# FFN's end with own buffers, and the first groups of a decoder-like layer in another order

## The chip, the cores and the metric

One core of a Trainium2 chip runs one program written by hand in Bass: every engine has its own list of instructions, and semaphores order them. The metric is the device time of one execution in microseconds.

## The reference

Input x is 32 sequences of 32 tokens of 256 values, 1024 rows in all; each sequence has a context of 257 rows of 256 values. Three layers are added to x in turn, each on layer-normalised rows:

```python
x = x + cross_attention(layernorm(x), ctx, ctx)   # one head: softmax(q k^T) v, q, k, v with biases
x = x + favor_attention(layernorm(x))             # 16 heads of 64, phi(x) = exp(x.W - |x|^2/2)/sqrt(128),
                                                  # causal within a sequence, divided by its sum, then Wo
x = x + ffn(layernorm(x))                         # gelu(bitlinear(x, w1)), bitlinear(., w2)
# bitlinear: activations rounded to 8 bits by their row's largest value, weights to -1, 0, 1 times a scale
```

## The kernel before, in words

The 1024 rows are 8 groups of 128 rows (NG = 8), four sequences in each. TensorE is called PE, VectorE DVE, ScalarE ACT, GpSimd POOL and the sync engine SP. The kernel has three parts: the front (cross attention of all groups, 0 to about 82 us), the middle (the features and products of the 16 heads) and the end (output projection and FFN).

**Front.** For each group g, with the lines at which its steps stand:

- `x_norm(g)` (DVE, L774) normalises x. For pairs of groups j, `xT(j)` transposes it (PE L1208), ACT takes the high part of the result (L493) and DVE the low part (L780), and `qk(j)` multiplies it with M = Wq Wk^T (PE L1220, copied by ACT L500). Products that need precision are made of three matmuls of high and low parts.
- `scores(g)` (PE L1242) multiplies with the context transposed (cT), `softmax_bias(g)` (DVE L834, three instructions from L837) takes the largest score, `exp(g)` (ACT L509), `pTt(g)` (PE L1255) transposes, `pTc(g)` (ACT L517) copies, `avm(g)` (PE L1276) multiplies with the context (cn), and `avc(g)` (DVE L842) adds the last key and copies. The four products of the last keys are `last_keys` (PE L1265).
- `avTt(g)`, `avT(g)` (PE L1287, ACT L523, DVE L827) transpose the result, `wv(g)` (PE L1295) multiplies it with Wv, and `x1(g)` (DVE L851) adds it to the rows kept in `res`. Into these POOL has added the bias bv (`add_bias`, L351) before.
- `stats(1, g)`, POOL's `rstd` (L358) and `x2_norm(g)` (DVE L857) normalise again. `nT(g)` (PE L1310, ACT, DVE) transposes, and `values(g, 0)` and `values(g, 1)` (PE L1319) make the two halves of the values of the next attention with the weight wv, whose high and low parts are `split_wv` (ACT L559) and `split_wv_low` (DVE L909).
- `t_bias(j)` (DVE L795) makes the scores' bias of the groups 2j and 2j+1, by two sums of products (L792) and an addition (L799). `softmax_bias` of these groups needs it.

The order is written out by hand in one loop per engine, in which step i stands for scores of group i with the later steps of the groups before it. Each engine does its list strictly in order. SP issues all loads in one queue (from L294); the buffers of the context are three deep (CB = 3), so the load of group g waits for the product of group g-3.

**End.** `layer1` makes the hidden rows, ACT the gelu, `quant_h` (DVE L1101) the scale, `round_h` (POOL L461) rounds into the one buffer `hr`, and `layer2` (PE L1597) multiplies with w2. For the last three groups (LATE = 5) PE transposes the rounded rows before they are cast (`late_hqTt`, L1583), and ACT writes the result into the one buffer `hqT` (`late_hqTc`, L698), group 7's in parts of its own (`hr_last`, `hqT_last`). `final(g)` (DVE L1121) writes the output rows into one of two buffers `fin`, group 7's in two halves (`final_last`, L1129), and SP stores them.

## Time and profile before

| | us |
|---|---|
| median of 3 timed runs | 250.89 (249.88 to 263.89) |
| the profiled execution | 249.94 |
| its span in the trace | 248.1 |
| PE busy | 237.8 (96%) |
| DVE busy | 183.3 (74%) |
| ACT busy | 145.6 (59%) |
| POOL busy | 100.2 (40%) |

The span runs from the first to the last instruction of the profiled execution; 1.8 us of its time lie around it. Matmuls are pipelined and their ends are modelled, so a row's time on PE may reach into the next; the distance from one start to the next is the price of one. Marks of time below are us from the start of the span.

### The profile page before, as it was taken

To read this page: it belongs to the slowest core of one execution; us is meant where nothing else is said; L and a number is where in the kernel's file an instruction comes from. 1 tells how busy PE (TensorE), PEld (TensorE's weight loads), DVE (VectorE), ACT (ScalarE), POOL (GpSimd) and SP (SyncE) were. 2 spreads that over 40 slices of the span, in tenths; PEclk is the share of its full clock that TensorE was granted. 3 is DMA by queue.
4 is the path that set the end of the run, shared out by engine and by line. 5 is a ranking of instruction groups with operands and counts; after the bars stand their busy time and mean duration, and the time that the engine had idled before them with its cause. 6 is when DMAs were issued, how large, how long until landed. Compare 5 with 4: busy or idle time off the path is not lost.

```text
span 248.1 us, 7008 instructions
## 1 busy us (share of the span) xinstructions
PE 237.8 (96%) x2736; PEld 189.0 (76%) x2736; DVE 183.3 (74%) x474; ACT 145.6 (59%) x285; POOL 100.2 (40%) x139
## 2 busy tenths in 40 slices
PE   8998889999999999999999999999999999999985
PEld 7954557786677777878787777878789988888855
DVE  5577888666843494978686776938488999999984
ACT  0454454454345788584857857485747257788772
POOL 2063113342302483828273494728820024444430
PEclk9999999999999999999999999999999999999999
DMA  6999999992044310100106000000000000000002
GB/s 176 370 385 405 396 395 396 338 397 78 1 169 151 105 42 4 45 0 4 45 5 211 1 3 0 5 0 4 3 3 3 3 1 3 21 21 24 22 24 66
DMA packets 15521, 26.83 MB, mean 108 GB/s; under 512 B 1248, under 2 KB 8832, under 8 KB 15488
## 3 DMA queue, kind: packets, MB, share of 16 engines
q1 hardware_dynamic: 14720, 25.96, 29.6%
q8 instruction: 22, 0.36, 0.6%
q10 hardware_dynamic: 768, 0.43, 0.6%
q14 instruction: 11, 0.09, 0.1%
HBM read 25.33 MB, written 1.05 MB: 106 GB/s over the span
## 4 chain that ended last, share of the span: by engine, by line
PE 46%; DVE 17%; POOL 16%; issue 11%; ACT 6%; DMA 3%; DVEq 0%; SPq 0%; POOLq 0%; ACTq 0%
PE b L1419 6%; POOL sq_lo L418 5%; POOL sq_sum L412 5%; PE b L1171 4%; PE b L1172 4%; PE b L1173 4%; PE b L1332 3%; PE b L1335 2%; PE b L1328 2%; DVE smk L976 2%; PE b L1472 2%; PE b L1571 2%; DMA xwk<-in_xWk 2%; DVE xn L792 2%; POOL wp_hi L385 2%
## 5 line engine op out<-in xcount | busy, mean ns | idle before, releaser
L902 DVE TENSOR_TENSOR x_lo<-b,x_hi 128x512 fp32r<-128x512 f32 x32 | 22.0, 691 | 24.5 <-ACT x_hi L490 24.1
L627 ACT ACTIVATE phi<-b 128x512 f32<-128x512 f32 x48 | 25.8, 602 | 14.5 <-PE b L1419 12.2
L418 POOL TENSOR_TENSOR sq_lo<-sq_sum,sq_hi 128x512 fp32r<-128x512 f32 x16 | 20.5, 1283 | 27.7 <-ACT sq_hi L490 27.7
L360 POOL TENSOR_TENSOR lnr<-lnv,mh 128x1 f32<-128x1 f32 x16 | 8.8, 551 | 55.0 <-DVE lnv L766 55.0
L412 POOL TENSOR_TENSOR sq_sum<-sq,sq 128x512 f32<-128x512 f32 x16 | 20.7, 1291 | 18.5 <-ACT sq L548 18.3
L1171 PE MATMUL b<-nT_lo,wp_hi 128*128 128x512 f32 x64 | 26.2, 409 | 0.5 <-POOL wp_lo L390 0.5
L1173 PE MATMUL b<-nT_hi,wp_hi 128*128 128x512 f32 x64 | 25.0, 391 | 0.0
L1172 PE MATMUL b<-nT_hi,wp_lo 128*128 128x512 f32 x64 | 25.0, 391 | 0.0
L548 ACT ACTIVATE sq<-b 128x512 f32<-128x512 f32 x32 | 19.7, 614 | 7.2 <-POOL sq_sum L412 4.8
L976 DVE TENSOR_TENSOR smk<-b,mask 64x512 f32<-64x512 f32 x32 | 21.9, 686 | 1.6 <-PE b L1438 0.4
L1472 PE MATMUL b<-va,smk 128*64 128x65 f32 x512 | 19.4, 225 | 0.8
L1472 PEld LDWEIGHTS b<-va,smk 128*64 128x64 f32 x512 | 16.7, 138 | 4.4 <-issue 2.5
L490 ACT ACTIVATE x_hi<-b 128x512 fp32r<-128x512 f32 x32 | 19.8, 618 | 0.0
L1171 PE MATMUL b<-wo_lo,yT_hi 128*128 128x256 f32 x64 | 18.9, 296 | 0.0
L1173 PE MATMUL b<-wo_hi,yT_hi 128*128 128x256 f32 x64 | 18.0, 281 | 0.0
L1172 PE MATMUL b<-wo_hi,yT_lo 128*128 128x256 f32 x64 | 18.0, 281 | 0.0
L1171 PEld LDWEIGHTS b<-nT_lo,wp_hi 128*128 128x128 f32 x64 | 12.0, 188 | 6.4 <-issue 3.0
L490 ACT ACTIVATE sq_hi<-sq_sum 128x512 fp32r<-128x512 f32 x16 | 10.2, 638 | 9.0 <-POOL sq_sum L412 8.9
L490 ACT ACTIVATE va<-b 128x512 f32<-128x512 f32 x16 | 9.5, 596 | 8.5 <-PE b L1335 8.5
L998 DVE TENSOR_TENSOR y<-b,rden 128x256 f32<-128x256 f32 x32 | 13.6, 425 | 1.1
L1173 PEld LDWEIGHTS b<-nT_hi,wp_hi 128*128 128x128 f32 x64 | 12.0, 188 | 2.6
L1172 PEld LDWEIGHTS b<-nT_hi,wp_lo 128*128 128x128 f32 x64 | 12.0, 188 | 2.2
(181 smaller groups left out, 617.3 us busy)
## 6 DMA issues: line engine op xcount, KB each, us to landing
cT<-in_ctxT SPq DMA_DIRECT2D x8, 1028.0 KB, 14.2
cn<-in_ctx SPq DMA_DIRECT2D x8, 1024.0 KB, 14.7
wv_raw<-in_aWv SPq DMA_DIRECT2D x1, 1024.0 KB, 13.8
wp_raw<-in_aWq SPq DMA_DIRECT2D x4, 256.0 KB, 5.2
wp_raw<-in_aWk SPq DMA_DIRECT2D x4, 256.0 KB, 5.2
w_raw<-in_w1T SPq DMA_DIRECT2D x1, 1024.0 KB, 4.8
w_raw<-in_w2T SPq DMA_DIRECT2D x1, 1024.0 KB, 5.5
wo<-in_aWo SPq DMA_DIRECT2D x1, 1024.0 KB, 5.8
```

Source lines behind the costliest of these rows:

```text
L412: nc.gpsimd.tensor_tensor(sq_sum[:], sq[0][:], sq[1][:], ALU.add).then_inc(sq_a, 1)
L418: nc.gpsimd.tensor_tensor(sq_lo[n % 2][:], sq_sum[:], sq_hi[n % 2][:].bitcast(F32), ALU.subtract).then_inc(sq_l, 1)
L490: return nc.scalar.activation(dst, src, ACT.Copy)
L548: nc.scalar.activation(sq[r][:], proj_bank(n, r), ACT.Square).then_inc(sq_f, 1)
L627: nc.scalar.activation(phi(n, a)[:], feature_bank(a), ACT.Exp).then_inc(f_exp, 1)
L902: nc.vector.tensor_tensor(x_lo[n % 3][r][:], proj_bank(n, r), x_hi[n % 3][r][:].bitcast(F32), ALU.subtract).then_inc(x_l, 1)
L976: nc.vector.tensor_tensor(smk[u % 2][keys, :, b, :], score_bank(u)[keys].rearrange("p (g n) -> p g n", n=PT), mask[keys].rearrange("p (a n ...
L1171: pe.matmul(acc, l_hi, r_lo, start=first, stop=False)
L1172: pe.matmul(acc, l_lo, r_hi, start=False, stop=False)
L1173: return pe.matmul(acc, l_hi, r_hi, start=False, stop=last)
L1419: mm = pe.matmul(feature_bank(a), w[rows], v[rows, :], start=(k == 0), stop=(k == len(terms) - 1))
L1472: mm = pe.matmul(value_bank(v)[PT * b:PT * (b + 1), g * VW:(g + 1) * VW], smk[u % 2][:, a * HALF + g, b, :], va[:, HALF * h + g, head, :], ...
```

## The change

- Loads: x comes in four transfers instead of three (groups 0-1, 2-3, 4-5, 6-7), wv in two halves; bv is issued by SP between cT and cn of group 1, no longer by ACT. ACT loads its activation table by a small instruction before it issues the transfers of the last keys.
- POOL: the reciprocal deviations of groups 4 and 5 come before the bias additions, and the addition of group 2 moves behind `x2_norm(0)`.
- Groups 0 to 2 are written out on PE, ACT and DVE. On PE `xT(2)` and `qk(2)` come before `scores(2)`, and `nT(1)` and `values(0, 1)` before `scores(3)`; `values(1, 0)` is cut in two around `wv(2)` and `pTt(3)`. On DVE `t_bias(1)` moves behind `avT(1)`, the statistics of groups 6 and 7 behind `avc(2)`.
- From group 3 on, on DVE: `avT(3)` comes before `softmax_bias(4)` and no longer behind it, `x_norm` of groups 6 and 7 moves from the end of step 3 behind `nT(2)` in step 4, and `avc` moves ahead of `t_bias` (in step 3 also ahead of `x2_norm`).
- End: group 6 gets its own buffers `hr_six` and `hqT_six`, so its rounding waits for its scale only. On PE the second part of its transposes moves ahead of the second half of `layer2(5)`, and `layer2(6)` is cut in two around the transposes of group 7. ACT issues the store of the first half of group 7.

```diff
@@ SP, loads @@
             load_weight(xwv, xWvT, ld_xwv)
+            load_x(2, 4, 6)
             load_cT(1)
-            load_x(2, 4, NG)
+            sp.dma_start(bvb[:], bv.rearrange("(a d) -> a d", a=1).broadcast_to([P, D])).then_inc(ld_bv, 16)
             load_cn(1)
+            load_wv(0)
             load_cT(2)
-            load_weight(wv_raw, aWv, ld_wv)
+            load_wv(1)
             load_cn(2)
+            load_x(3, 6, NG)
@@ SP, the last stores @@
-            for half in range(2):
-                cols = slice(P * half, P * (half + 1))
-                sp.wait_ge(fin_r, NG + half)
-                sp.dma_start(outv[LAST][:, cols], fin[LAST % 2][:, cols]).then_inc(stored_last, 16)
+            sp.wait_ge(fin_r, NG + 1)
+            sp.dma_start(outv[LAST][:, P:D], fin[LAST % 2][:, P:D]).then_inc(stored_last, 16)
@@ POOL @@
-            for g in range(3):
+            x_rstd(2)
+            for g in range(2):
                 add_bias(g)
-            x_rstd(2)
...
                 if g == 0:
+                    add_bias(2)
                     add_bias(3)
@@ POOL, round_h @@
                 if 1 <= g <= LATE:
                     pool.wait_ge(hq_r, g)
-                elif g > LATE:
-                    pool.wait_ge(hT_mm, 2 * (g - LATE))
@@ ACT @@
+            act.wait_ge(setup_dve, 1)
+            copy(spare[:], mh[:, 0:2])
             last = ctx[:, 2 * P, :].rearrange("(g b) d -> b g d", b=BG)
...
@@ ACT, late_hqTc @@
-                if g < LAST:
+                if g == LATE:
                     act.wait_ge(f2_mm, g)
@@ ACT, end @@
             late_hqTc(LAST, 0)
+            act.wait_ge(fin_r, NG)
+            act.dma_start(out.rearrange("(g p) d -> g p d", p=P)[LAST][:, 0:P], fin[LAST % 2][:, 0:P]
+                          ).then_inc(stored_last, 16)
@@ DVE, groups 0 to 2 written out @@
+            xT(1)
+            avc(0)
+            dve.wait_ge(ld_x[2], 16)
+            stats(0, 4, 6)
+            softmax_bias(1)
+            avT(0)
+            x_norm(4)
+            x_norm(5)
+            inverse_sum(1)
+            residual(0)
+            avc(1)
+            x2_norm(0)
+            xT(2)
+            avT(1)
+            t_bias(1)
+            split_wv_low(0, 0)
+            split_wv_low(0, 1)
+            nT(0)
+            softmax_bias(2)
+            residual(1)
+            inverse_sum(2)
+            x2_norm(1)
+            split_wv_low(1, 0)
+            split_wv_low(1, 1)
+            nT(1)
+            avc(2)
+            dve.wait_ge(ld_x[3], 16)
+            stats(0, 6, 8)
@@ PE, end @@
             late_hqTt(LATE, 1)
             layer2(LATE, 0)
             late_hqTt(LAST - 1, 0)
+            late_hqTt(LAST - 1, 1)
             layer2(LATE, 1)
-            late_hqTt(LAST - 1, 1)
+            layer2(LAST - 1, 0)
             late_hqTt(LAST, 0)
             late_hqTt(LAST, 1)
-            layer2(LAST - 1)
+            layer2(LAST - 1, 1)
             layer2_last()
```

PE around the scores of group 3. The row `cT_87,qkT_135` is `scores(3)`, `cn_92,pT` is `avm(2)`, `xn_1_142` is `nT(1)`, rows with `wv_hi` or `wv_lo` are `values`. Before:

```order
L1283 MATMUL b<-cn_92,pT 32x256 x8
L1251 MATMUL b<-cT_87,qkT_135 32x257 x8
L1292 MATMUL b<-ident,av 128x128 x2
L1316 MATMUL b<-ident,xn_1_142 128x128 x2
L1328 MATMUL b<-wv_hi,nT_hi 128x512 x2
L1332 MATMUL b<-wv_lo,nT_hi 128x512 x2
L1335 MATMUL b<-wv_hi,nT_lo 128x512 x2
```

Now:

```order
L1317 MATMUL b<-cn_92,pT 32x256 x8
L1350 MATMUL b<-ident,xn_1_142 128x128 x2
L1362 MATMUL b<-wv_hi,nT_hi 128x512 x2
L1366 MATMUL b<-wv_lo,nT_hi 128x512 x2
L1372 MATMUL b<-wv_hi,nT_lo 128x512 x2
L1285 MATMUL b<-cT_87,qkT_135 32x257 x8
L1326 MATMUL b<-ident,av 128x128 x2
L1362 MATMUL b<-wv_hi,nT_hi 128x512 x2
```

The transpose and the value half of an earlier group moved ahead of the scores; behind them now stands the first part of the next value half.

DVE from `x2_norm(2)` (`xn_0_141`) to `nT(2)`. The two `ISA xn,sm` rows are the sums of `t_bias(2)`, `av<-cl` is `avc(3)`, `xn<-res` is `x_norm` of groups 6 and 7, `sm<-b` opens `softmax_bias(4)`. Before:

```order
L771 TENSOR_SCALAR xn_0_141<-res,lnm,lnr 128x256
L792 ISA xn,sm<-xn,v1b 128x256
L792 ISA sm 128x1
L792 ISA xn,sm<-xn,v1b 128x256
L792 ISA sm 128x1
L799 TENSOR_SCALAR sm<-sm,v1b 128x2
L848 SCALAR_TENSOR_TENSOR av<-cl,prob_138,b 128x256
L771 TENSOR_SCALAR xn<-res,lnm,lnr 128x256 x2
L837 TENSOR_REDUCE sm<-b 128x1
L838 TENSOR_TENSOR sm<-sm 128x1
L839 TENSOR_TENSOR sm<-sm 128x1
L831 TENSOR_TENSOR avT_lo<-b,avT_hi 128x256
```

Now:

```order
L865 SCALAR_TENSOR_TENSOR av<-cl,prob_138,b 128x256
L788 TENSOR_SCALAR xn_0_141<-res,lnm,lnr 128x256
...
L816 TENSOR_SCALAR sm<-sm,v1b 128x2
L848 TENSOR_TENSOR avT_lo<-b,avT_hi 128x256
L854 TENSOR_REDUCE sm<-b 128x1
L855 TENSOR_TENSOR sm<-sm 128x1
L856 TENSOR_TENSOR sm<-sm 128x1
L881 TENSOR_TENSOR nT_lo<-b,nT_hi 128x2x128
L788 TENSOR_SCALAR xn<-res,lnm,lnr 128x256 x2
```

`avc(3)` moved to the front, `avT(3)` ahead of the softmax bias, and the normalising of groups 6 and 7 from ahead of that bias to behind `nT(2)`.

PE at the end. `hr` are the transposes of groups 5 and 6, `w2q` with x4 a half of `layer2`. Before:

```order
L1593 MATMUL b<-ident,hr 128x128 x4
L1612 MATMUL b<-w2q,hqT 128x256 x4
L1593 MATMUL b<-ident,hr 128x128 x4
L1612 MATMUL b<-w2q,hqT 128x256 x4
L1593 MATMUL b<-ident,hr 128x128 x4
L1593 MATMUL b<-ident,hr_last 128x128 x8
L1612 MATMUL b<-w2q,hqT 128x256 x8
L1623 MATMUL b<-w2q,hqT_last 128x128 x16
```

Now:

```order
L1649 MATMUL b<-ident,hr 128x128 x4
L1668 MATMUL b<-w2q,hqT 128x256 x4
L1649 MATMUL b<-ident,hr_six 128x128 x8
L1668 MATMUL b<-w2q,hqT 128x256 x4
L1668 MATMUL b<-w2q,hqT_six 128x256 x4
L1649 MATMUL b<-ident,hr_last 128x128 x8
L1668 MATMUL b<-w2q,hqT_six 128x256 x4
L1679 MATMUL b<-w2q,hqT_last 128x128 x16
```

Both parts of group 6's transposes now stand together, and half of its `layer2` moved ahead of group 7's transposes.

## Rows read from the trace of the kernel before

**Rows 1.** The page, parts 1 and 2: busy time, and granted clock in 40 slices.
```profile
PE 237.8 (96%) x2736; PEld 189.0 (76%) x2736; DVE 183.3 (74%) x474; ACT 145.6 (59%) x285; POOL 100.2 (40%) x139
PEclk9999999999999999999999999999999999999999
```

**Rows 2.** Stretches: length, then busy us of PE, PEld, DVE, ACT, POOL; clock, DMA share, GB/s.
```profile
18.79:25.27 6.48, 5.26 (x48) 2.97 (x51) 5.00 (x18) 2.78 (x7) 2.39 (x4) 1.00 1.03 403
25.27:32.73 7.46, 6.12 (x58) 3.61 (x50) 6.18 (x21) 4.15 (x9) 1.03 (x2) 1.00 1.04 395
32.73:41.12 8.39, 8.24 (x69) 5.88 (x73) 6.93 (x20) 3.86 (x10) 2.60 (x5) 1.00 1.04 400
41.12:47.96 6.84, 6.71 (x65) 4.90 (x61) 4.82 (x15) 2.99 (x8) 1.35 (x3) 1.00 1.07 342
...
55.58:62.12 6.54, 6.27 (x60) 4.47 (x56) 4.27 (x15) 2.69 (x7) 1.65 (x4) 1.00 0.25 89
```

**Rows 3.** Timeline of PE: start, us, instruction, idle time before it and its releaser.
```profile
22.32 0.51 PE L1307 MATMUL b<-xwv_hi,avT_lo 128*128 128x256 f32 x2 [0.75 <-DVE avT_lo L831]
...
29.02 0.51 PE L1262 MATMUL b<-ident,prob 128*128 128x128 f32 x2 [0.46 <-ACT prob L514]
...
32.73 1.07 PE L1251 MATMUL b<-cT,qkT 128*32 128x257 f32 x16 [0.63 <-DMA cT<-in_ctxT]
```

**Rows 4.** Timeline of PE: from qk(3) to pTt(5), and two value halves.
```profile
51.54 0.40 PE L1231 MATMUL b<-xT_hi,m_hi 128*128 128x256 f32 x2
...
52.95 0.41 PE L1262 MATMUL b<-ident,prob 128*128 128x128 f32 x2
...
72.90 0.62 PE L1328 MATMUL b<-wv_hi,nT_hi 128*128 128x512 f32 x2
...
74.30 0.63 PE L1328 MATMUL b<-wv_hi,nT_hi 128*128 128x512 f32 x2
```

**Rows 5.** Timeline of DVE: t_bias(0) first and last, then from t_bias(2) to nT(2).
```profile
11.41 0.42 DVE L792 CUSTOM_DVE_ANT_0 xn<-xn,v1b 128x256 f32<-128x256 f32 x1
...
12.23 0.23 DVE L799 TENSOR_SCALAR sm<-sm,v1b 128x2 f32<-128x2 f32 x1
...
39.82 0.42 DVE L792 CUSTOM_DVE_ANT_0 xn<-xn,v1b 128x256 f32<-128x256 f32 x1
...
41.76 0.48 DVE L848 SCALAR_TENSOR_TENSOR av<-cl,prob,b 128x256 f32<-128x256 f32 x1
42.16 0.73 DVE L771 TENSOR_SCALAR xn<-res,lnm,lnr 128x256 f32<-128x256 f32 x2
42.81 0.42 DVE L837 TENSOR_REDUCE sm<-b 128x1 f32<-128x257 f32 x1
...
43.88 0.41 DVE L864 TENSOR_TENSOR nT_lo<-b,nT_hi 128x256 fp32r<-128x256 f32 x1
```

**Rows 6.** Timeline of POOL beside t_bias(2).
```profile
39.98 1.72 POOL L356 TENSOR_TENSOR res<-res,bvb 128x256 f32<-128x256 f32 x2 [0.60 <-DVE xn L771]
```

**Rows 7.** The issue of cT of group 3 on SP, and its us to landing.
```profile
15.02 2.87 SPq L275 DMA_DIRECT2D cT<-in_ctxT  x1
...
cT<-in_ctxT SPq DMA_DIRECT2D x1, 1028.0 KB, 17.7
```

**Rows 8.** Timelines of the tail by engine, and the last stores' us to landing.
```profile
240.05 1.12 POOL L467 TENSOR_SCALAR hr<-hid,qsc 128x1024 f32<-128x1024 f32 x1 [2.76 <-PE b L1593]
...
241.22 0.66 PE L1593 MATMUL b<-ident,hr 128*128 128x128 f32 x4 [0.91 <-POOL hr L467]
...
244.33 1.06 PE L1623 MATMUL b<-w2q,hqT_last 128*128 128x128 bf16 x16
...
242.62 0.47 DVE L1126 SCALAR_TENSOR_TENSOR fin<-b,qsc,res 128x256 f32<-128x256 f32 x1
...
245.30 0.61 DVE L1136 SCALAR_TENSOR_TENSOR fin<-b,qsc,res 128x128 f32<-128x128 f32 x2 [0.28 <-DMA out<-fin]
...
out<-fin SPq DMA_DIRECT2D x2, 64.0 KB, 1.6
```

More of the change, by code:

```diff
@@ L172, in build @@
         hqT = z3.take("hqT", [P, HC, P], BF16)
+        hr_six = z3.take("hr_six", [P, HID])
+        hqT_six = z3.take("hqT_six", [P, HC, P], BF16)
         hr_last = z3.take("hr_last", [P, HID])
@@ L577, in _ @@
             qk(0)
-            for i in range(NG + 1):
-                if 0 <= i - 1:
-                    avT(i - 1)
-                if 0 <= i - 2:
+            exp(0)
+            pTc(0)
+            xT(1)
+            clcopy(0)
+            clcopy(1)
+            qk(1)
+            avT(0)
+            exp(1)
+            pTc(1)
+            xT(2)
+            clcopy(2)
+            clcopy(3)
+            avT(1)
+            split_wv(0)
+            nT(0)
+            qk(2)
+            exp(2)
+            pTc(2)
+            split_wv(1)
+            vcopy(0, 0)
+            nT(1)
+            vcopy(0, 1)
+            for i in range(3, NG + 1):
+                avT(i - 1)
+                if i >= 4:
                     nT(i - 2)
-                if i == 2:
-                    split_wv(0)
                 if i == NG:
@@ L913, in split_wv_low, with residual @@
                                         ALU.subtract).then_inc(wv_l, 1)
-            for i in range(NG + 1):
-                if i == 2:
+            def residual(g):
+                settle()
+                x1(g)
+                dve.wait_ge(x1_cp, g + 1)
+                stats(1, g, g + 1)
+            softmax_bias(0)
+            x_norm(2)
+            x_norm(3)
+            inverse_sum(0)
+            xT(1)
+            avc(0)
+            dve.wait_ge(ld_x[2], 16)
+            stats(0, 4, 6)
+            softmax_bias(1)
+            avT(0)
+            x_norm(4)
[4 more added lines that the diff above has]
+            x2_norm(0)
+            xT(2)
+            avT(1)
+            t_bias(1)
+            split_wv_low(0, 0)
+            split_wv_low(0, 1)
+            nT(0)
+            softmax_bias(2)
[4 more added lines that the diff above has]
+            split_wv_low(1, 1)
+            nT(1)
+            avc(2)
+            dve.wait_ge(ld_x[3], 16)
+            stats(0, 6, 8)
+            for i in range(3, NG + 1):
+                if i == 4:
                     avT(i - 1)
@@ L1336, in values @@
                 mm.then_inc(v_mm, 1)
+            def values(g, hh):
+                values_high(g, hh)
+                values_low(g, hh)
             def project(n, *rs):
@@ L1364, in _ @@
             pe.wait_ge(u_cp, 1)
-            for i in range(NG + 1):
+            scores(0)
+            last_keys(0)
+            last_keys(1)
+            pTt(0)
+            xT(1)
+            avm(0)
+            qk(1)
+            scores(1)
+            avTt(0)
+            last_keys(2)
+            wv(0)
+            pTt(1)
+            xT(2)
+            avm(1)
+            last_keys(3)
+            avTt(1)
+            qk(2)
+            nT(0)
+            wv(1)
+            scores(2)
+            values(0, 0)
+            pTt(2)
+            avm(2)
+            nT(1)
+            values(0, 1)
+            for i in range(3, NG + 1):
                 if i < NG:
                     scores(i)
-                if i == 0:
-                    last_keys(0)
-                    last_keys(1)
                 if i == NG:
```

134 lines of the change are left out of this document (49 added, 85 removed).

## Prediction

> **What bounds the kernel now.** I read the page first: TensorE (PE) is busy 96% of the span and its granted clock is full in all 40 slices [rows 1]. So only PE's gaps can be won, and the question for every edit is whether it closes one. The reader then cuts the front into stretches from one group's scores to the next [rows 2]: in the stretches that begin at 18.79 and 25.27 us, PE is busy 5.26 of 6.48 and 6.12 of 7.46 us, so 1.22 and 1.34 us idle; behind them the stretches are nearly full (0.15, 0.13 and 0.27 us idle in those from 32.73, 41.12 and 55.58). The timeline of PE says who ended the gaps [rows 3]: VectorE's (DVE's) avT_lo (0.75 us at 22.32), ScalarE's softmax (0.46 at 29.02), and the landing of cT of group 3 (0.63 at 32.73). These are waits for a chain: scores, softmax bias on DVE, exponential on ACT, transpose, copy, product. It is late because DVE does something else first. Behind 82 us nothing of the change touches the middle, which shifts as a block. The tail [rows 8] is another chain: DVE's final of group 5 at 242.62, its store, and DVE's final of group 7 at 245.30, which waited 0.28 us for that store.
>
> **The front, step by step.** I write scores(g), softmax(g) and so on for a group's steps; a group has 128 rows. Nothing changes ahead of scores(1) at 18.79 us. All marks below are sums of durations of the profile, in its time.
>
> 1. t_bias(1) leaves its place ahead of softmax(1). It goes behind avT(1). In the trace t_bias costs two very different prices [rows 5]: t_bias(0) runs from 11.41 to 12.46 us (1.05 us), t_bias(2) from 39.82 to 41.76 (1.94), and beside the second lies GpSimd's pair of bias additions, 39.98 to 41.70 [rows 6]. So it is 1.05 us alone and 1.9 us beside GpSimd. The page SBUF — State Buffer (section SBUF: two separate sides) of the Trainium skill says that VectorE with two SBUF inputs and GpSimd exclude each other from a shared port pair for a whole instruction; the trace agrees in direction (1.05 against 1.94 us). By that rule every step that reads two tensors in SBUF would be dear beside add_bias, which is what I assume for t_bias(2) and half of t_bias(1) anyway. With it gone, DVE is ready when scores(1) ends, at 19.85, instead of 21.1 us; avT(0) follows at 20.7, the wait of 0.75 us goes, pT(1) comes at 21.65, the product avm(1) at 22.5 instead of 24.4 (cn of group 1 has to be there; below). Of those 1.9 us some 0.85 is one product of the last keys that PE now does behind it.
>
> 2. PE does xT(2) and qk(2) before scores(2), and nT(1) and values(0,1) before scores(3). A half of values is 1.40 us (72.90 to 74.30), qk is 1.41 us (51.54 to 52.95) [rows 4]. In the kernel before, PE waited for cT of group 3 with that work undone; now it fills the time. No work is added or removed, so what counts is the start of scores(4), before which both kernels have done the same work: 41.12 us before. My walk: qk(2) ends at 26.0; scores(2) starts at 26.9; DVE is at t_bias(1) from 25.7 to 27.1 (half of it beside add_bias: I take 1.4, bounds 1.05 and 2.17), wv_lo of the first half until 28.35, nT(0), softmax(2) from 28.7 to 29.5. values(0,0) waits 0.5 us for wv_lo, pT(2) waits 0.8 us and comes at 30.1, avm(2) runs from 30.85 to 31.75, and values(0,1) waits 0.6 us for the second wv_lo pair, which can't start before x2_norm(1) at 31.95. It ends at 34.15 and scores(3) starts there. From there to scores(4) PE has 4.4 us of work (the stretch of 8.39 us [rows 2] less 3.0 for qk(2), values(0,1) and nT(1), which are done, less about 1.0 of short waits that its order leaves out) and about 0.1 of waits. scores(4) starts at 38.65: 2.5 us earlier. Bounds: 0.4 (t_bias(1) at 2.17, and the short waits of each step 0.2 longer than I have them) and 4.2 us (no wait left).
>
> 3. Then DVE is the late one. Before, DVE normalised groups 6 and 7 at 42.16 us, ahead of softmax(4) at 42.81 [rows 5], and xT(3) never waited. Now avc(3) and x2_norm(2) come first, then t_bias(2), avT(3), softmax(4), nT(2) and only then x_norm of 6 and 7, and PE's xT(3) needs both. From the end of avm(3) at 38.7: avc 0.45, x2_norm 0.4, t_bias(2) 1.94 (add_bias(4) and (5) again follow x2_norm(2) and lie beside it), avT(3), softmax(4) and nT(2) 1.45 (42.81 to 44.26, the same three in another order), x_norm twice 0.7: xT(3) starts at 43.75. PE is ready for it at 42.2. That is a new wait of 1.5 us, against 0.13 us idle in that stretch before. What queues behind it on PE: pT(4), values(2,0), avm(4), scores(5). scores(5) starts at 46.75, 1.2 us earlier than the 47.96 of before. So of 2.5 us 1.3 are given back. Bounds of the loss: 0.4 (t_bias(2) at 1.05) and 1.7.
>
> 4. In group 5 avc(5) comes before t_bias(3). Before, avT of group 5 waited behind it, part of the 0.27 us idle in the stretch from 55.58 [rows 2]; now PE passes, and t_bias(3) delays softmax(6) by 1 to 2 us, which PE covers with two value halves. I take 0.3 us won, bounds -0.3 and 0.5.
>
> 5. Transfers. The queue is full until the last context: 395 to 403 GB/s in the first three stretches of [rows 2], and cT of group 3, issued at 15.02, landed 17.7 us later, at 32.7 [rows 7]. The order changes, the bytes ahead of cT(3) do not: x in three parts and bv (128 KB, now on SP's queue instead of ACT's) lie ahead as before. Ahead of cT of group 2 there is 0.25 MB more, 0.6 us: 25.5, needed at 26.9. wv comes in halves, the first at about 23, the second at about 27, both before ACT wants them (25.3 and 30.8). The cost is 0; the cover is 1.4 us at each. Against it speaks the page DMA: Bandwidth & Descriptors (section Measured) of the Trainium skill: batch to 1 MiB, a 1 MB transfer moves at 341 GB/s and 64 KB at 138. By that rule two more transfers would put cT(3) about 1 us later, at 33.8, still ahead of 34.15. The trace gives this little weight: several transfers are in flight at once (each takes some 17 us to land), and the rate hardly moves from stretch to stretch.
>
> 6. The table load of ACT now lies ahead of the clc transfers, and m_hi waited for PE anyway: 0.
>
> My walk leaves out the short bubbles between steps, so I take 0.1 us off: front 1.2 + 0.3 - 0.1 = 1.4 us.
>
> **The tail.** Rounding of group 6 no longer waits for PE's transposes of group 5: GpSimd starts at 239.05 instead of 240.05 [rows 8], PE's wait of 0.9 us goes, the last products start at 243.6 instead of 244.33. But the final of group 7 writes the buffer from which group 5 is stored, and that store follows final(5) at 242.62, which stands behind DVE's rounding of group 7; nothing of this moves. It still starts at 245.3. So this edit is worth 0 us by itself, because the store takes the place of the wait removed (bounds 0 and 0.3). The first half of the last store now goes out on ACT's queue, so SP issues the second at once: 0.1 to 0.2 us, with 1.6 us to landing as before [rows 8].
>
> Sum: 249.94 (the profiled execution; its span is 248.14 and 1.8 lies around it) - 1.4 - 0.15 = 248.4 us. The three timed runs had a median of 250.89, 0.95 above the profiled one, and 249.88 as the fastest: the sum stands against the fast ones, and the upper end of the range leaves room for that.
>
> **Rivals.**
> - Given back in full (249.8 us, chance 0.20). The gain at scores(4) is only as large as the new wait at xT(3), 1.3 us. For it: DVE works 6.18 of 7.46 and 6.93 of 8.39 us in the two stretches [rows 2], so it has little room to be early. Against it: t_bias(1), the step that made DVE late for group 1, is out of the way.
> - No new wait (246.8 us, chance 0.13). avm(3) is early enough or t_bias(2) costs 1.05 us, so that x_norm is done within 0.3 us of PE's need; 248.4 - 1.5. Against it: add_bias(4) is released by x2_norm(2) as before.
> - Slower (250.8 us, chance 0.12). DVE's queue bounds the front: t_bias(1) at 2.17 us pushes wv_lo, softmax(2) and the second wv_lo pair, and scores(4) starts at 40.7 instead of 41.12, then the wait at xT(3) takes 1.3: +0.9. It decides as soon as scores(4) wins less than 1.3 us. For it: wv_lo is now waited for twice by PE.
> - Transfers slip (249.2 us, chance 0.05), if the split ones cost over 1 us ahead of cT(3); each us behind 34.15 is lost.
> - The tail gives its 0.7 us in full (247.7, chance 0.05), if final(5) moves too. Nothing in DVE's order says so.
>
> **How the numbers follow.** My own case holds 0.45, from 247.6 to 249.2. 2% of this kernel is 5 us, about what a measurement of it can tell from no change; the idle time of PE in the whole front is about 3 us [rows 2], so faster by over 2% has 0.03 and slower 0.02, for something I don't see; within 2% has 0.95. The range goes from 246.4 (no new wait, and the whole of step 4) to 251.0 (the slower rival, or the forecast with timed runs as high as the median above).
>
> **What would show it.** Right: scores(4) near 38.7 and xT(3)'s transposes waiting over a microsecond for DVE's xn near 43; scores(5) near 46.8; t_bias(1) between 1.05 and 1.5 us; final of group 7 still waiting for the store near the same distance behind final(5), with PE's last products 0.7 us earlier. Wrong: no wait at xT(3), scores(4) above 40 us, a wait of PE for cT or cn, or a front won that doesn't reach 82 us.

## The result and the profile after

| | before | changed |
|---|---|---|
| median of 7 timed runs | 249.91 us (249.59 to 263.89) | 248.26 us (247.97 to 248.97) |
| the profiled execution, its span | 249.94, 248.1 us | 248.59, 246.8 us |

The ratio is 0.9934, with a 95% interval from 0.9912 to 0.9956: 1.65 us faster. (One execution of the kernel before took 263.89 us, 5% more than the others; the medians don't hang on it.) The forecast was 248.4. As will be seen, the number came out, and so did the two places on which it rests, a gain up to scores(4) and a new wait at xT(3) that takes most of it back. Their difference did not: the front won about half of what was forecast for it, and other places made up for it. Nor did the reasons: two of the steps credited with the gain cost nothing when they are put back, and the one priced at zero, the order of the loads, is a condition of it.

The stretches of the changed kernel between the starts of scores(1), (2), (3), (4), (5) and (7), columns as in [rows 2]:

```profile
18.64:27.34 8.70, 8.69 (x74) 5.93 (x73) 6.62 (x23) 5.33 (x12) 4.06 (x6) 1.00 1.04 392
27.34:34.53 7.19, 6.21 (x49) 3.35 (x49) 6.25 (x18) 3.27 (x8) 0.56 (x1) 1.00 1.05 397
34.53:39.23 4.70, 4.70 (x50) 3.15 (x52) 3.05 (x13) 2.53 (x6) 0.72 (x2) 1.00 1.03 393
39.23:47.43 8.20, 7.00 (x65) 4.96 (x60) 6.38 (x20) 2.88 (x8) 3.28 (x5) 1.00 1.06 353
47.43:61.24 13.81, 13.81 (x128) 10.34 (x124) 8.66 (x30) 6.55 (x17) 4.61 (x10) 1.00 0.74 279
```

The second number, PE's busy time, fills the first, third and fifth stretch to 0.01 us. Up to scores(4) PE idles 0.01 + 0.98 us, where it was 1.22 + 1.34 + 0.15 [rows 2]. The fourth stretch idles 1.20, where it was 0.13. These are the waits of PE there, and where scores(4) now starts:

```profile
31.13 1.07 PE L1317 MATMUL b<-cn,pT 128*32 128x256 f32 x16 [0.47 <-ACT pT L498]
...
33.40 0.73 PE L1366 MATMUL b<-wv_lo,nT_hi 128*128 128x512 f32 x2 [0.36 <-DVE wv_lo L929]
...
39.23 1.05 PE L1285 MATMUL b<-cT,qkT 128*32 128x257 f32 x16
...
44.33 0.66 PE L1250 MATMUL b<-ident,xn 128*128 128x128 f32 x4 [1.20 <-DVE xn L788]
```

Neither avT_lo nor cT(3) is waited for any more [rows 3]. In their place stand short waits for pT(2) and wv_lo, and one of 1.20 us at xT(3). DVE and POOL in front of that one:

```profile
40.20 0.42 DVE L809 CUSTOM_DVE_ANT_0 xn<-xn,v1b 128x256 f32<-128x256 f32 x1
...
40.55 0.95 DVE L809 CUSTOM_DVE_ANT_0 xn<-xn,v1b 128x256 f32<-128x256 f32 x1
...
41.54 0.58 DVE L816 TENSOR_SCALAR sm<-sm,v1b 128x2 f32<-128x2 f32 x1
...
43.54 0.73 DVE L788 TENSOR_SCALAR xn<-res,lnm,lnr 128x256 f32<-128x256 f32 x2
```

```profile
40.36 1.73 POOL L365 TENSOR_TENSOR res<-res,bvb 128x256 f32<-128x256 f32 x2 [0.60 <-DVE xn L788]
```

The second sum of products of t_bias(2), 40.55 to 41.50, lies inside the two additions and costs 0.95 us, the first, which began before them, 0.42. t_bias(2) takes 1.92 us, from 40.20 to 42.12.

Starts in profiled executions differ already at scores(1) (17.93 to 18.79 us over all runs of this study; more on this under step 6). So the table below counts from scores(1). By that count scores(4) is 1.74 us earlier than before (20.59 against 22.33), scores(5) 0.38 (28.79 against 29.17), scores(7) 0.73 (42.60 against 43.33). The forecast had 2.5 at scores(4), 1.2 at scores(5) and 1.4 for the whole front.

The tail, DVE's rows of the last finals:

```profile
241.82 0.47 DVE L1160 SCALAR_TENSOR_TENSOR fin<-b,qsc,res 128x256 f32<-128x256 f32 x1
243.31 0.47 DVE L1160 SCALAR_TENSOR_TENSOR fin<-b,qsc,res 128x256 f32<-128x256 f32 x1
244.14 0.61 DVE L1170 SCALAR_TENSOR_TENSOR fin<-b,qsc,res 128x128 f32<-128x128 f32 x2 [0.36 <-DMA out<-fin]
```

From final(5) to final(7) it is 2.32 us; it was 2.68 [rows 8]. The last one waits for the store of group 5 as before, and that store landed in 1.7 us. So the 1.35 us between the two profiled executions are 0.15 at scores(1), 0.73 up to scores(7), 0.28 up to final(7) (0.36 behind final(5), less 0.08 lost ahead of it), and about 0.2 in the last store.

### The profile page after: what moved, and what is told of

Read it like the earlier page. It is cut to its first block, busy times and chain, and to the rows that moved or that the text cites. A ratio compares the mean times of both kernels' runs of the same rounds, so it can differ in the third digit from the quotient of the medians.

```text
span 246.8 us, 7010 instructions
## 1 busy us (share of the span) xinstructions
PE 237.9 (96%) x2736; PEld 188.2 (76%) x2736; DVE 181.4 (73%) x474; ACT 146.4 (59%) x286; POOL 99.7 (40%) x139
## 3 DMA queue, kind: packets, MB, share of 16 engines
HBM read 25.33 MB, written 1.05 MB: 107 GB/s over the span
## 4 chain that ended last, share of the span: by engine, by line
PE 51%; POOL 15%; DVE 13%; issue 11%; ACT 6%; DMA 3%; SPq 0%; DVEq 0%; POOLq 0%; ACTq 0%
PE b L1475 6%; POOL sq_lo L428 5%; POOL sq_sum L422 5%; PE b L1205 4%; PE b L1206 4%; PE b L1207 4%; PE b L1317 3%; PE b L1366 3%; PE b L1372 3%; PE b L1362 2%; PE b L1285 2%; DVE smk L1010 2%; PE b L1528 2%; PE b L1627 2%; DMA xwk<-in_xWk 2%
## 6 DMA issues: line engine op xcount, KB each, us to landing
wv_raw<-in_aWv SPq DMA_DIRECT2D x2, 512.0 KB, 13.8
```

## Experiments: the wait at xT(3) and the tail

Each of these four is the changed kernel with one edit. The kernel before, timed beside them, had a median of 249.86 us.

**x_norm of groups 6 and 7 a step earlier** (DVE, the stretch behind softmax(3)).

```diff
-                if i == 4:
+                if i == 3:
                     x_norm(6)
                     x_norm(7)
```

> The changed kernel with one edit: DVE normalises x of groups 6 and 7 in step 3 behind avT(3-1), ahead of residual(2), where it sat idle for 0.86 us waiting for wv(2). Theory (DVE's queue gives back 1.3 us at xT(3)): the wait of PE of 1.20 us for DVE's xn at 44.33 goes to 0.0 to 0.3 us, PE next waits up to 0.4 us for the exponential of group 4, scores(5) starts 0.7 to 1.0 us earlier than 47.43, and the time is 0.7 to 1.0 us below the changed kernel's (247.3 to 247.6). Rival (the wait at xT(3) only stands in for another limit, such as t_bias(2) ahead of softmax(4)): the time drops by less than 0.3 us.

Measured 247.49 us, ratio 0.9905 (0.9883 to 0.9926). The wait at xT(3) is gone, and a smaller one comes up behind it:

```profile
43.27 0.50 PE L1296 MATMUL b<-ident,prob 128*128 128x128 f32 x2 [0.38 <-ACT prob L522]
```

From scores(4) to scores(5) it is 7.44 us instead of 8.20. So taking away the wait at xT(3) is worth 0.8 us, not 1.2, because 0.38 us come back at the next wait, and the time fell by 0.77.

**POOL's additions of groups 4 and 5 a step later.**

```diff
-                if 2 <= g < 4:
-                    add_bias(2 * g)
-                    add_bias(2 * g + 1)
+                if g == 3:
+                    for k in range(4, NG):
+                        add_bias(k)
```

> The changed kernel with one edit: POOL adds the bias to groups 4 and 5 one step later, beside those of groups 6 and 7, so nothing of POOL lies beside t_bias(2). Theory (t_bias costs 1.05 us alone and 1.95 beside POOL's additions): t_bias(2) takes 1.0 to 1.15 us, PE's wait at xT(3) falls from 1.20 to 0.3 to 0.5 us, scores(5) starts 0.7 to 0.9 us earlier. Rival (the price belongs to the place in DVE's order or to the data, not to POOL): t_bias(2) stays at 1.8 to 2.0 us and the wait at 1.2.

Measured 247.15 us, ratio 0.9895 (0.9880 to 0.9911). Nothing on DVE was moved, and this is what t_bias(2) became:

```profile
39.73 0.42 DVE L809 CUSTOM_DVE_ANT_0 xn<-xn,v1b 128x256 f32<-128x256 f32 x1
...
40.08 0.42 DVE L809 CUSTOM_DVE_ANT_0 xn<-xn,v1b 128x256 f32<-128x256 f32 x1
...
40.54 0.23 DVE L816 TENSOR_SCALAR sm<-sm,v1b 128x2 f32<-128x2 f32 x1
...
42.20 0.73 DVE L788 TENSOR_SCALAR xn<-res,lnm,lnr 128x256 f32<-128x256 f32 x2
```

and of the wait at xT(3):

```profile
42.98 0.66 PE L1250 MATMUL b<-ident,xn 128*128 128x128 f32 x4 [0.47 <-DVE xn L788]
```

t_bias(2) takes 1.04 us instead of 1.92, and PE waits 0.47 us instead of 1.20. So it is shown that the price of t_bias is POOL's company, and that this company makes 0.7 us of the wait at xT(3). The stretch took 7.32 us, 0.88 less. The time fell by 1.11, somewhat more than the trace accounts for (scores(7) is 0.85 earlier).

**An output buffer of its own for group 7.**

```diff
+        fin_last = z3.take("fin_last", [P, D])
...
-                    dve.wait_ge(stored[LAST % 2], 16 * (LAST // 2))
```

> The changed kernel with one edit: group 7's output rows get a buffer of their own, so final(7) does not wait for the store of group 5. Theory (in the tail the store hides what PE wins): final of group 7's first half starts when PE's product is there, 1.7 to 2.0 us behind final(5) instead of 2.32, and the time falls by 0.2 to 0.5 us. Rival (the tail is set by PE or DVE themselves): no change beyond 0.1 us.

Measured 247.86 us, ratio 0.9925 (0.9909 to 0.9941): 0.4 below the changed kernel, with intervals that overlap. The trace shows the wait gone:

```profile
242.69 0.48 DVE L1161 SCALAR_TENSOR_TENSOR fin<-b,qsc,res 128x256 f32<-128x256 f32 x1
243.26 0.80 DVE L1170 SCALAR_TENSOR_TENSOR fin_last<-b,qsc,res 128x128 f32<-128x128 f32 x2
```

final(5) started at 241.21, so final(7) follows it by 2.05 us and no longer by 2.32. These 0.27 us are the part that the trace shows.

**The front alone:** the changed kernel with the tail of before (one `hr`, one `hqT` for groups 5 and 6, both last stores by SP).

```diff
                 if 1 <= g <= LATE:
                     pool.wait_ge(hq_r, g)
+                elif g > LATE:
+                    pool.wait_ge(hT_mm, 2 * (g - LATE))
...
-                if g == LATE:
+                if g < LAST:
                     act.wait_ge(f2_mm, g)
...
-            late_hqTt(LAST - 1, 1)
             layer2(LATE, 1)
-            layer2(LAST - 1, 0)
+            late_hqTt(LAST - 1, 1)
             late_hqTt(LAST, 0)
             late_hqTt(LAST, 1)
-            layer2(LAST - 1, 1)
+            layer2(LAST - 1)
```

> The changed front with the tail of the kernel before (one buffer for groups 5 and 6, old order on PE, both last stores on SP). Theory (the tail is worth 0.1 to 0.2 us): time within 0.3 us above the changed kernel's, 248.3 to 248.6. Rival (the tail carries a part that I had put down to a shorter store, final(7) 2.32 instead of 2.68 us behind final(5)): 0.5 us or more above, and final(7) at 2.6 us or more behind final(5) again.

Measured 248.44 us (247.98 to 249.94, 10 runs), ratio 0.9940 (0.9913 to 0.9967), 0.18 above the changed kernel. The tail edit is worth a few tenths at most, and these runs can't tell it from nothing. The profiled execution was one of the longest:

```profile
244.96 0.61 DVE L1171 SCALAR_TENSOR_TENSOR fin<-b,qsc,res 128x128 f32<-128x128 f32 x2 [0.92 <-DMA out<-fin]
```

The store of group 5 took 2.7 us here, and final(7) came 3.33 us behind final(5). In the kernel before this store took 2.1 us (2.68 behind), in the changed one 1.7 (2.32 behind). So the store's own time moves the end by more than the edit does. How little the edit does is seen in the run with the loads alone (below): it has the old tail and a store of 1.7 us, and final(7) follows final(5) by 2.36 us. So of the 0.36 us between 2.68 and 2.32 only some 0.04 are the edit's.

## Experiments: where the gain in front of scores(4) comes from

Most of these undo one part of the front. The first three undo what the prediction had as the source of the gain, and cost nothing. The kernel before had a median of 249.86 us beside four of them, and of 249.96 us beside the other four (t_bias(1) and POOL's order back, only x as before, only the new loads, groups 0 to 2 back).

**t_bias(1) back ahead of softmax(1).**

```diff
+            t_bias(1)
             softmax_bias(1)
...
             avT(1)
-            t_bias(1)
```

> The changed kernel with one step put back: t_bias(1) again stands ahead of softmax_bias(1) on DVE instead of behind avT(1). Theory 1 (this step is the source of the gain at scores(4)): softmax(1) comes 1.3 to 1.9 us later, PE waits about 0.8 us for avT_lo of group 0 again and avm(1) and what follows come 1 us later, while the waits of 0.36 and 0.47 us around wv_lo and pT(2) get shorter by 0.4 together; scores(4) is at least 0.5 us later counted from scores(1), and the time is 248.8 to 249.2. Rival (PE's new order alone makes the gain; qk(2), nT(1) and values(0,1) fill whatever wait there is): scores(4) stays within 0.2 us, time 248.1 to 248.4.

Measured 248.23 us, ratio 0.9928 (0.9910 to 0.9946): nothing lost. DVE's rows in front of softmax(1):

```profile
18.61 0.43 DVE L809 CUSTOM_DVE_ANT_0 xn<-xn,v1b 128x256 f32<-128x256 f32 x1
...
18.96 0.42 DVE L809 CUSTOM_DVE_ANT_0 xn<-xn,v1b 128x256 f32<-128x256 f32 x1
...
19.43 0.23 DVE L816 TENSOR_SCALAR sm<-sm,v1b 128x2 f32<-128x2 f32 x1
19.69 0.43 DVE L854 TENSOR_REDUCE sm<-b 128x1 f32<-128x257 f32 x1
```

Here t_bias(1) stands behind the statistics of groups 4 and 5 (in the kernel before it stood ahead of them). It costs 1.05 us and ends about when scores(1) does, so softmax(1) starts 1.27 us behind the start of scores(1), against 1.14 in the changed kernel. Before, t_bias(1) took 2.1 us.

**t_bias(1) and POOL's order back.** This time t_bias(1) stands ahead of the statistics of 4 and 5, as in the kernel before.

```diff
+            for g in range(3):
+                add_bias(g)
             x_rstd(2)
-            for g in range(2):
-                add_bias(g)
...
                 if g == 0:
-                    add_bias(2)
                     add_bias(3)
...
             avc(0)
+            t_bias(1)
             dve.wait_ge(ld_x[2], 16)
...
             avT(1)
-            t_bias(1)
```

> The changed kernel with t_bias(1) back in its old place and POOL's order of before as well (bias additions of groups 0 to 2 ahead of the reciprocal deviations of 4 and 5). With t_bias(1) alone back it ran in 1.05 us beside an idle POOL and was done before scores(1) ended. Theory 1' (what made t_bias(1) harmful is POOL's order: three additions beside it make it 2.1 us, and softmax(1) starts 1 us late): t_bias(1) about 2 us, softmax(1) 0.8 to 1.3 us behind the end of scores(1), a wait for avT_lo near 0.8 us, time 248.6 to 249.2. Rival (PE's new order covers that too): 248.1 to 248.4.

Measured 248.24 us, ratio 0.9935 (0.9917 to 0.9954): a miss for Theory 1', and the row on POOL says why.

```profile
18.34 2.10 POOL L365 TENSOR_TENSOR res<-res,bvb 128x256 f32<-128x256 f32 x3 [1.40 <-DMA bvb<-in_bv]
```

The three additions can't start, because bv now comes tenth on SP's queue and not early on ACT's. t_bias(1) was over at 18.32. So the collision of before has been taken away more than once, by t_bias's place and by bv's landing. The changed kernel with bv on ACT's queue again was not tried, so what the place of t_bias(1) would be worth there is open.

**nT(1) and values(0,1) back behind scores(3)**, on three engines; PE's part:

```diff
             avm(2)
-            nT(1)
-            values(0, 1)
...
-                if i >= 4:
-                    nT(i - 2)
-                    values(i - 3, 1)
+                nT(i - 2)
+                values(i - 3, 1)
```

> The changed kernel with nT(1) and values(0,1) back behind scores(3), as before, on PE, ACT and DVE; xT(2) and qk(2) stay ahead of scores(2), and t_bias(1) in its new place. Theory 1 (step 2: the work stands where PE would wait for cT of group 3): PE waits 0.5 to 1.5 us for cT(3), which lands at about 32.7, and scores(4) is 0.5 to 1.2 us later counted from scores(1): 248.7 to 249.4. Rival (the order only moves the wait; behind avm(2) PE waits for wv_lo anyway, and scores(3) early lets DVE begin softmax(3) early): scores(4) within 0.2 us, 248.0 to 248.4.

Measured 248.30 us, ratio 0.9936 (0.9918 to 0.9954). PE's waits in that stretch:

```profile
31.09 1.07 PE L1311 MATMUL b<-cn,pT 128*32 128x256 f32 x16 [0.47 <-ACT pT L498]
...
32.71 1.07 PE L1279 MATMUL b<-cT,qkT 128*32 128x257 f32 x16 [0.54 <-DMA cT<-in_ctxT]
...
39.09 1.05 PE L1279 MATMUL b<-cT,qkT 128*32 128x257 f32 x16
```

PE waits 0.54 us for cT(3), and no longer 0.36 for wv_lo: one short wait for another, and scores(4) comes 20.51 us behind scores(1) instead of 20.59. The rival's reading holds.

**The loads as before**, all engines' orders as changed.

```diff
-            load_x(2, 4, 6)
             load_cT(1)
+            load_x(2, 4, NG)
...
-            load_wv(0)
             load_cT(2)
-            load_wv(1)
+            load_weight(wv_raw, aWv, ld_wv[0])
             load_cn(2)
-            load_x(3, 6, NG)
```

> The changed kernel with the loads as they were: x of groups 4 to 7 in one transfer behind cT(1), wv in one transfer behind cT(2); the engines' orders stay. Theory 1 (step 5: the order of transfers costs and gives nothing, bytes ahead of cT(3) are the same): within 0.2 us of the changed kernel, 248.1 to 248.5, with no new wait of PE. Rival (the parts matter, since wv now is wanted by values(0,1) ahead of scores(3)): whole wv lands about 1.5 us later than its first half does, ACT's split_wv(0) at about 25 us and DVE's wv_lo wait for it, scores(2) to scores(4) come 0.5 to 1 us later: 248.7 to 249.3.

Measured 249.93 us, ratio 1.0002 (0.9993 to 1.0012). The whole gain is gone, more than even the rival gave. DVE:

```profile
19.29 0.75 DVE L777 BATCH_NORM_STATS2 lns<-res 128x6 f32<-128x256 f32 x2 [1.58 <-DMA res<-in_x]
...
20.43 0.42 DVE L853 TENSOR_REDUCE sm<-b 128x1 f32<-128x257 f32 x1
...
21.49 1.38 DVE L787 TENSOR_SCALAR xn<-res,lnm,lnr 128x256 f32<-128x256 f32 x2
```

and ACT:

```profile
27.39 1.06 ACT L496 ACTIVATE wv_hi<-wv_raw 128x1024 fp32r<-128x1024 f32 x1 [0.85 <-DMA wv_raw<-in_aWv]
28.36 0.36 ACT L496 ACTIVATE nT_hi<-b 128x256 fp32r<-128x256 f32 x1
28.62 0.83 ACT L512 ACTIVATE qkT<-b,bqk 128x256 f32<-128x256 f32 x2
```

The x of groups 4 to 7 in one piece lands at 19.3, where the first half alone landed at 14.8. DVE's queue stands still for it 1.58 us, so softmax(1) is 0.65 late. POOL's additions slip with it onto x_norm of 4 and 5, which takes 1.38 us instead of 0.72, and PE waits 0.52 for that. Then ACT stands still 0.85 us for wv, and nT(0) and the copies of qk(2) are queued behind it. scores(2) needs those copies: 9.57 us behind scores(1) instead of 8.70. (bv stays on SP's queue in this run, and the table load early.)

**Only x as before, wv in halves.** (The lines of x above, without those of wv.)

> The changed kernel with x of groups 4 to 7 in one transfer behind cT(1), but wv still in two halves. The run with both put back lost 1.67 us (249.93), with two delays in its trace: statistics of 4 and 5 blocked 1.58 us by x in front of softmax(1), and ACT blocked 0.85 us by wv in front of nT(0) and qk(2). Theory X (x is the one that counts; DVE's queue stands still in front of softmax(1), and POOL's additions are pushed beside x_norm of 4 and 5): 248.9 to 249.4, the rest is wv's. Rival W (wv in halves is the whole of it, the delay by x is caught up): 248.1 to 248.5.

Measured 248.76 us, ratio 0.9948 (0.9929 to 0.9967), between the two theories: 0.5 of the 1.67 us hangs on x, the rest on wv or on both together. In its trace DVE waits 0.46 us for x, PE 0.57 for avT_lo, and ACT nowhere for wv. The way from the one to the other leads over POOL:

```profile
20.24 1.41 POOL L364 TENSOR_TENSOR res<-res,bvb 128x256 f32<-128x256 f32 x2
```

```profile
19.86 0.42 DVE L853 TENSOR_REDUCE sm<-b 128x1 f32<-128x257 f32 x1 [0.35 <-PE b L1283]
20.32 0.66 DVE L854 TENSOR_TENSOR sm<-sm 128x1 f32<-128x1 f32 x1
21.01 0.65 DVE L855 TENSOR_TENSOR sm<-sm 128x1 f32<-128x1 f32 x1
```

softmax(1) starts 1.14 us behind scores(1), as in the changed kernel. But POOL's additions, which follow the statistics of 4 and 5, now lie beside both of its short steps, and these take 0.66 and 0.65 us. In the changed kernel they take 0.16 and 0.60. wv whole with x in parts was not tried.

**Only the new loads** (with ACT's table load), on the kernel before: the lines above the other way round, bv on SP's queue and the early table load.

```diff
+            act.wait_ge(setup_dve, 1)
+            copy(spare[:], mh[:, 0:2])
...
-            act.dma_start(bvb[:], bv.rearrange("(a d) -> a d", a=1).broadcast_to([P, D])).then_inc(ld_bv, 16)
```

> The kernel before with nothing but the new loads: x in four transfers, wv in two halves, bv on SP between cT(1) and cn(1), and ACT's table load ahead of its transfers. Putting the loads back in the changed kernel cost the whole gain (249.93), so two readings are open. Theory A (the loads win by themselves: earlier x and wv shorten waits of any order): about 248.3, at most 248.8. Theory B (they win nothing where nothing asks for x(4,5) before 20 us and wv before 27 us, and are only the condition of the new order of groups 0 to 2): 249.6 to 250.1, with the waits of PE for avT_lo, prob and cT of the kernel before still in the trace.

Measured 250.37 us, ratio 1.0016 (0.9998 to 1.0035): nothing won. Theory B holds in the time, but not in all of its waits. PE's:

```profile
25.52 1.07 PE L1261 MATMUL b<-cT,qkT 128*32 128x257 f32 x16 [0.92 <-DMA cT<-in_ctxT]
...
32.85 1.07 PE L1261 MATMUL b<-cT,qkT 128*32 128x257 f32 x16 [0.51 <-DMA cT<-in_ctxT]
```

The wait for avT_lo ahead of scores(2) is gone (t_bias(1) took 1.38 us here, not 2.1), and one of 0.92 us for cT(2) stands in its place.

**Groups 0 to 2 in the order of before**, all else as changed; PE's part:

```diff
+            last_keys(3)
             pTt(1)
-            xT(2)
             avm(1)
-            last_keys(3)
+            scores(2)
             avTt(1)
-            qk(2)
             nT(0)
             wv(1)
-            scores(2)
+            xT(2)
+            pTt(2)
             values(0, 0)
-            pTt(2)
             avm(2)
-            nT(1)
-            values(0, 1)
```

> The changed kernel with groups 0 to 2 in the order of before on PE, ACT and DVE (t_bias(1), xT(2), qk(2), nT(1) and values(0,1) in their old places); loads, POOL, the order from group 3 on and the end as changed. Putting back t_bias(1) alone (248.23) or nT(1) and values(0,1) alone (248.30) cost nothing. Theory B (the order of groups 0 to 2 and the loads win only together; what carries it is xT(2) and qk(2) ahead of scores(2), which fills PE while cT(3) is under way until 32.7 us): scores(3) waits over 1 us for cT(3), scores(4) is 1 to 1.8 us later counted from scores(1), the time 249.3 to 250.0. Rival (the gain is the loads' and POOL's and the new order of DVE from group 3 on): 248.1 to 248.6.

Measured 250.70 us, ratio 1.0023 (1.0006 to 1.0041), 2.4 us above the changed kernel. PE:

```profile
24.89 1.07 PE L1278 MATMUL b<-cT,qkT 128*32 128x257 f32 x16 [0.92 <-DMA cT<-in_ctxT]
...
28.59 0.51 PE L1289 MATMUL b<-ident,prob 128*128 128x128 f32 x2 [0.37 <-ACT prob L522]
32.25 1.07 PE L1278 MATMUL b<-cT,qkT 128*32 128x257 f32 x16 [0.53 <-DMA cT<-in_ctxT]
...
45.96 0.66 PE L1243 MATMUL b<-ident,xn 128*128 128x128 f32 x4 [1.19 <-DVE xn L783]
```

The wait for avT_lo that stood before scores(2) in the kernel before is not there either, but scores(2) comes no earlier for it: it waits 0.92 us for cT(2), and scores(3) 0.53 for cT(3). Theory B is right in its direction and short in its size: the wait for cT(3) is not over 1 us, but scores(4) is 1.94 us later and the time 0.7 above its range. This kernel also keeps the wait at xT(3), 1.19 us, without the gain that paid for it.

**The three edits that helped, together.** (x_norm early, POOL late, own buffer; their diffs are above.)

> Three edits on the changed kernel at once: x_norm of groups 6 and 7 ahead of residual(2) (alone 247.49), POOL's bias additions of groups 4 to 7 behind x2_norm(3) (alone 247.15), and an output buffer of its own for group 7 (alone 247.86). Theory 1: the first two remove the same wait of 1.2 us at xT(3), so their gains (0.77 and 1.11) do not add, and together they give at most 1.2; the third adds its 0.4 at the other end: 246.5 to 246.8. Rival (they are independent and all add): 248.26 - 0.77 - 1.11 - 0.40 = 246.0.

Measured 246.79 us (246.46 to 246.99), ratio 0.9874 (0.9858 to 0.9889): 1.5 us below the changed kernel, and the fastest of this study. The time fits Theory 1, its reason doesn't. From scores(4) to scores(5) it is 6.63 us, 1.57 less than in the changed kernel, where the first two edits alone gave 0.76 and 0.88. So in this stretch they add up, and to more than the 1.2 that the theory allowed. Each alone leaves another short wait, for the exponential (0.38) or for xn (0.47). With both, PE waits for neither:

```profile
42.43 0.60 PE L1250 MATMUL b<-ident,xn 128*128 128x128 f32 x4
42.87 0.40 PE L1296 MATMUL b<-ident,prob 128*128 128x128 f32 x2
```

In the medians the gains of the three (0.77, 1.11, 0.40) come to 2.28 us, and together they gave 1.47. Two of them are larger than what their traces show (0.85 at scores(7), 0.27 at final(7)); the median of four runs isn't sharp enough to say more.

All in one table, us from the start of scores(1) to that of scores(4), (5) and (7) in the profiled execution, and the median (the kernel before had 249.86 to 249.96):

| kernel | scores(4) | scores(5) | scores(7) | time |
|---|---|---|---|---|
| before | 22.33 | 29.17 | 43.33 | 249.86 |
| changed | 20.59 | 28.79 | 42.60 | 248.26 |
| x_norm early | 20.62 | 28.06 | 41.87 | 247.49 |
| POOL late | 20.61 | 27.93 | 41.75 | 247.15 |
| t_bias(1) back | 20.55 | 28.76 | 42.58 | 248.23 |
| and POOL back | 20.67 | 28.87 | 42.69 | 248.24 |
| values(0,1) back | 20.51 | 28.71 | 42.52 | 248.30 |
| x whole | 21.12 | 29.32 | 43.14 | 248.76 |
| loads back | 22.02 | 30.23 | 44.04 | 249.93 |
| loads alone | 23.02 | 29.85 | 44.01 | 250.37 |
| groups 0-2 back | 22.53 | 30.74 | 44.55 | 250.70 |
| best | 20.60 | 27.23 | 41.05 | 246.79 |

At scores(4), ahead of the new wait, the two halves of the change are seen apart: the loads alone are 0.69 us later than the kernel before, the orders with the old loads 0.31 earlier, and both together 1.74 earlier.

## Why the prediction was right in its number, and wrong in its reasons

**How the number came out.** The forecast took 1.4 us from the front and 0.15 from the tail. Between the two profiled executions 1.35 us are gone, and only 0.73 of them lie between scores(1) and scores(7). Another 0.15 came ahead of scores(1), 0.32 from a store that happened to land sooner, and 0.15 to 0.2 from the last store, the part that was forecast. So the hit at 248.4 is in good part luck: the mis-sized term is step 2's, 2.5 us at scores(4), of which 1.74 came, while the loss behind it was sized right (1.3 forecast, 1.36 measured). Counted at scores(5), 0.38 us were left of 1.2, nearer to the rival "given back in full" than to the forecast. The medians differ by 1.65 us, 0.3 more than the two profiles; no trace assigns these 0.3, but step 6 names a place that could hold them.

**What bounds the front.** The prediction named the landing of cT(3) as one of three gaps. It is more. In every kernel with PE's old order of groups 0 to 2, scores(3) starts at 32.3 to 32.9 us, on that landing, whatever was won ahead of it; scores(2) stands at 24.9 to 25.5 in the same way. (In the kernel before, cT(2) was issued at 9.98 and landed 14.9 later, at 24.9, just ahead of scores(2) at 25.27.) From the landing of cT(3) on, all that is left to do before scores(4) counts in full: 8.39 us before, 6.38 in the run with values(0,1) back. The new order wins because 1.4 us of it, qk(2), is now done ahead, while the transfer is under way. The other 0.6 us are short gaps: values(0,1) took 1.83 us before and 1.48 in that run, wv(2) 0.97 and 0.74. That qk(2) carries the gain is reached by elimination (t_bias(1) and values(0,1) put back cost nothing, all of groups 0 to 2 put back costs 2.4 us); xT(2) and qk(2) were not moved alone, and the rest of the order of groups 0 to 2, on DVE and ACT above all, was not separated from them.

**Step 1 (t_bias(1) out of softmax(1)'s way): the cause was wrong.** Its marks came out: avT_lo is not waited for, and the product avm(1) starts at 22.67 (forecast 22.5), t_bias(1) took 1.04 us at 26.08 (priced 1.4, lower bound 1.05). But put back it costs nothing in this kernel, with POOL's order of before too. What I took for the price of the place was the price of its company: 2.1 us beside three additions, 1.05 alone. And alone it fits, but for 0.1 us, into the 0.90 us for which DVE stands idle ahead of softmax(1) in the changed kernel. Even a won wait would not have counted by itself: with the new loads and the old order avT_lo's wait disappears ahead of scores(2), and cT(2)'s, 0.92 us, takes its place. I saw this pair of prices and used it for the price of the step, not for the question of what else would make it cheap.

**Step 2 (PE's order): half right.** The forecast was scores(4) at 38.65, 2.5 us earlier; it came at 39.23, 1.89 earlier in the profile's time and 1.74 counted from scores(1). scores(2) at 27.34 (forecast 26.9), avm(2) at 31.13 (30.85) and scores(3) at 34.53 (34.15) are each 0.3 to 0.4 us later, and the last stretch took 4.70 us (4.5). The waits for pT(2) and wv_lo are there with 0.47 and 0.36 us. For moving qk(2) the reason holds; for values(0,1), which I counted along with it ("now it fills the time"), it doesn't: it covers a wait of 0.54 us for cT(3), and what that gives goes into a wait of 0.36 for wv_lo and the short gaps around it.

**Step 3 (DVE late, 1.3 given back): right.** The wait is 1.20 us (forecast 1.5: PE was ready at 43.13, 0.9 later than I walked it, DVE at 44.33, 0.6 later), and 1.36 us are given back (8.20 against 6.84). Of the two runs made for it, one took the wait away by the order, and the other cut it to 0.47 by POOL alone. The bound "0.4 with t_bias(2) at 1.05" became 0.48 in the latter (7.32 against 6.84).

**Step 4 (avc(5) ahead of t_bias(3)): right,** 0.3 forecast, 0.35 measured: from scores(5) to scores(7) 13.81 us instead of 14.16. It is 14.16 with the loads alone, which have the old order there, and 13.81 with groups 0 to 2 back, which have the new.

**Step 5 (transfers, cost 0): this is the step that failed.** As a cost it was right: the wv halves landed at 22.5 and 26.4 (forecast 23 and 27), cT(3) at 32.4, at 392 to 397 GB/s (395 to 403 before). So the sentence from the Trainium skill, DMA: Bandwidth & Descriptors (section Measured), by which parts below 1 MiB would be slower, has no support here. Its figures are for transfers issued from GpSimd, and these went out on SP's queue with several under way. (The "some 17 us" that each transfer was said to take is cT(3)'s 17.7. cT(2) took 14.9, wv 13.8, x of groups 4 to 7 12.7.) But I asked only what the new loads cost, and not what the new order would be without them. The new order wants x(4) and x(5) at 17.7 us and wv at 25.6, where the old loads deliver at 19.3 and 27.4. In the time, loads alone give nothing, orders alone nothing, both 1.6 us. At scores(4) the same three give -0.7, 0.3 and 1.7 us. My sum gave all of it to the orders and could be right only because both were in the change.

**Step 6 (table load, 0)** was not tried by itself, and 0 may be too little. In the profile of before the load ended at 8.24 us and PE's product at 8.31, and ACT went on at 8.35. In the 13 profiles with the early load ACT waits for that product alone, and goes on between 7.46 and 8.27 us, in the middle one at 7.91. In 11 of the 13, and in the kernel before, scores(1) follows 10.4 us behind that. With the load in its old place ACT could not have used a product that is ready before 8.24. That gives an estimate of about 0.3 us for the early load in a middling execution (8.24 less 7.91). It leans on a single profile of the kernel before. Why the product itself is done sooner or later is not taken apart.

**The tail, 0.15: right within what can be told.** The last products started 1.3 us earlier (243.00 against 244.33), 0.5 more than final(5) did, and the store took the wait's place as forecast. With a buffer of its own for group 7 the median is 0.4 us lower, without the tail edit 0.2 higher; neither is clear of the noise.

**The rivals.** "Given back in full" missed the difference of 1.74 won and 1.36 lost, 0.38 us. "Slower" needed t_bias(1) at 2.17 us; it was 1.04. "Transfers slip" needed cT(3) behind 34.15; it landed at 32.4. "The tail in full" needed an earlier final(5); it moved with the front (0.80 us earlier). "No new wait" (246.8) did not happen. It took 1.5 us off the forecast where step 3 had only 1.3 given back. The best kernel comes to the same number, 246.79, by edits of its own, one of which is in the tail.

## What to carry to other kernels

Where a change has a part that "costs nothing", ask also what the other parts would be without it: a new order of the work and the order of its loads are one edit, and neither half shows the gain in the time. Check a forecast at marks inside the kernel as well as at its end: here the end agreed within 0.2 us, and the front was off by half of its gain. On a path that waits for a stream of transfers at several places, count the work that is left behind each landing; only what moves ahead of a landing wins, and closing a wait ahead of it only makes the next one longer. A step that is slow in one place may be slow for its company; look for another engine's rows beside it before moving it, because moving the company may be cheaper (here one `if` on POOL: 1.1 us in the time, 0.9 in the trace).
